# A graph layer with routed experts on one core: VectorE's chains reordered and shortened, block numbers loaded two at a time, TensorE's order kept

## What is computed

```
n = layernorm(x)
summed = segment_sum(n[src], dst);  deg = count of edges into a node
z = concat([n, summed / max(deg, 1)]) @ gnn_weight          # 512 -> 256
x1 = x + z / norm(z) + gnn_bias
h = layernorm(x1);  probs = softmax(h @ gate_w + gate_b);  e = argmax(probs)
pos = running count of the nodes that chose e;  kept = pos < 977
y = (relu(h @ w1[e] + b1[e]) @ w2[e] + b2[e]) * probs[e] * kept
out = x1 + nan_to_num(y)
```

## Time and profile before

| | us |
|---|---|
| median of 3 runs (lowest to highest) | 1400.24 (1398.0 to 1404.33) |
| profiled execution | 1398.44 |
| its span in the trace | 1396.6 |
| PE busy / DVE busy / POOL busy / ACT busy | 1120.8 / 868.0 / 907.4 / 464.5 |
| trips 0 to 7 (start of the first row store to that of the ninth) | 89.3 to 282.0 |
| trips with quads and a chunk | about 261 to 1245 |
| late trips, then trips with a chunk alone | to 1310, to 1396.6 |

### The profile page before, as it was taken

The page is one execution under the profiler, slowest core; times in us unless marked ns, Lnnn a source line. Parts: engine busy times, 40 slices in busy tenths (PEclk is TensorE's granted clock), DMA queues, the critical chain, the costliest instruction groups (busy, mean ns, idle before and its releaser), DMA issues.

```text
span 1396.6 us, 29269 instructions
## 1 busy us (share of the span) xinstructions
PE 1120.8 (80%) x4989; PEld 820.2 (59%) x4990; DVE 868.0 (62%) x3856; ACT 464.5 (33%) x1360; POOL 907.4 (65%) x931
## 2 busy tenths in 40 slices
PE   1076766788889898989888898989898888887786
PEld 1054554566666666666666666666666666654454
DVE  8645454666666666666666666666666666665443
ACT  3511212233333333333333333333333333334342
POOL 3167676677777777777777777777777777731101
PEclk9999798999999999999999999999999999999999
DMA  7686878443444434343433434343434344321111
GB/s 246 199 269 206 249 226 243 148 127 116 131 123 123 130 118 133 115 132 114 128 115 112 121 110 121 110 126 110 125 110 121 114 113 120 113 75 43 47 38 35
DMA packets 113601, 183.38 MB, mean 131 GB/s; under 512 B 21419, under 2 KB 84448, under 8 KB 113584
## 3 DMA queue, kind: packets, MB, share of 16 engines
q0 software_dynamic: 43328, 109.52, 27.2%
q1 hardware_dynamic: 70256, 73.69, 17.6%
HBM read 155.29 MB, written 35.83 MB: 137 GB/s over the span
## 4 chain that ended last, share of the span: by engine, by line
DVE 29%; PE 27%; DVEq 20%; issue 18%; DMA 3%; ACT 2%; ACTq 0%; SPq 0%; POOLq 0%; POOL 0%
PE ps_q L726 14%; PE ps_h L792 7%; DVE sel L1037 6%; DVEq L1301 6%; PE ps_t L800 2%; PE ps_b L811 2%; DVE acc L1046 2%; DVEq L1108 2%; DVEq L894 2%; DMA b_b<-in_L_ffn_b 2%; DVEq L1037 1%; DVEq L1064 1%; DVE row L1150 1%; DVE idx L1033 1%; DVE bn L1156 1%
## 5 line engine op out<-in xcount | busy, mean ns | idle before, releaser
L461 POOL DMA_INDIRECT ring<-xn_d,idx x784 | 788.0, 1005 | 316.5 <-issue 171.5
L726 PE MATMUL ps_q<-ring,sel 128*128 128x257 f32 x1952 | 582.8, 405 | 151.2 <-DVE sel L1037 119.9
L726 PEld LDWEIGHTS ps_q<-ring,sel 128*128 128x128 f32 x1952 | 346.5, 195 | 291.5 <-issue 234.3
L1037 DVE SCALAR_TENSOR_TENSOR sel<-lane,block,dst_t 128x512 f32<-128x512 bf16 x245 | 184.3, 752 | 132.8 <-issue 76.6
L811 PE MATMUL ps_b<-w_sb,hid_t 128*128 x832 | 213.8, 385 | 16.1 <-ACT hid_t L626 16.1
L1046 DVE TENSOR_TENSOR acc<-acc,ps_q 128x257 f32 x245 | 103.2, 421 | 178.4 <-issue 166.9
L792 PE MATMUL ps_h<-w_sb,hid_t 128*128 x416 | 200.0, 608 | 6.2 <-ACT hid_t L594 6.2
L811 PEld LDWEIGHTS ps_b<-w_sb,hid_t 128*128 128x128 f32 x832 | 153.5, 190 | 49.0 <-issue 30.1
L621 ACT ACTIVATE hid<-ps_h 128x512 f32<-128x512 f32 x104 | 62.1, 597 | 190.4 <-PE ps_h L792 190.4
L626 ACT ACTIVATE hid_t<-ps_t,b_t 128x128 f32<-128x128 f32 x416 | 113.2, 383 | 31.5 <-PE ps_t L800 31.5
L792 PEld LDWEIGHTS ps_h<-w_sb,hid_t 128*128 128x128 f32 x416 | 75.5, 191 | 67.4 <-issue 65.2
(11 more groups left out here) (194 smaller groups left out, 1230.0 us busy)
## 6 DMA issues: line engine op xcount, KB each, us to landing
w_sb<-in_L_ffn_w SPq DMA_DIRECT2D x32, 512.0 KB, 9.7
ring<-xn_d,idx POOLq DMA_INDIRECT x784, 2.8
disp_d<-hid SPq DMA_DIRECT2D x8, 1040.0 KB, 7.9
xs<-disp_d SPq DMA_DIRECT2D x53, 130.0 KB
ys<-disp_d SPq DMA_DIRECT2D x53, 130.0 KB
b_b<-in_L_ffn_b SPq DMA_DIRECT2D x53, 128.0 KB
xb<-in_x SPq DMA_DIRECT2D x51, 128.0 KB
out<-row SPq DMA_DIRECT2D x51, 128.0 KB
```

The source lines that it names most:

```text
L461: pool.indirect_dma_start(ring[:, (k % 2) * TQ + j, 0:D], None, xn_d[:, :], bass.IndirectOffsetOnAxis(ap=idx[:, k * TQ + j:k * TQ + j + 1] ...
L726: mm = pe.matmul(ps[:, 0:AW], sel[:, s, j, :], ring[:, (k % 2) * TQ + j, 0:AW], start=(j == 0), stop=(j == TQ - 1), skip_group_check=True)
L1037: dve.scalar_tensor_tensor(out=sel[:, s, :, :], in0=lane[:, :].rearrange("p (j m) -> p j m", j=1).to_broadcast((P, TQ, P)), scalar=block0[ ...
```

## The change

Work is moved between VectorE and ScalarE, and within VectorE's order. `plan`, TensorE's order of steps, keeps its entries, but for the loads of block numbers.

- `finish_row` leaves `result` and goes, with `choose`, into one set of chains with `new_row`, behind `select_quad`(3). `route` is alone behind `select_quad`(1), `result` alone behind `select_quad`(2).
- `down` waits for a new semaphore `count_read`, which the second step of `finish_row` raises, in place of `row_ready`.
- `route` has 5 steps in place of 9 (negated logits, the winner by the minimum before the exponentials), `result` 7 in place of 8 (the bias is scaled by ScalarE, `out_bias`), `new_row` loses its correction step: ScalarE's `row_norm` does that in four small operations. The copy of `row` to `sent` and the conversion of the edge indices `idx` go to ScalarE (`exponent`, `gather_rows`); VectorE's `quad_rows` goes.
- Each engine loads two block numbers for a quad: VectorE behind each selection, TensorE at one step of each quad.
- ScalarE prepares the next node block at the end of its trip, ahead of the copy that `gate` waits for; the normalised rows get a tile of their own, `xl`.
- In trips with a chunk alone ScalarE's `out_bias` stands between the two `hidden` copies.

```diff
             def exponent(t):
...
+                act.activation(sent[:, :], row[:, :], ACT.Copy).then_inc(exp_ready, 1)
...
-            def trip(t, chunk=True):
+            def trip(t, chunk=True, next_known=None):
                 c = chunks(t)
-                act.load([blk], ntab[0:1, ds(t, 1)])
                 act.wait_ge(xl_ps, t + 1)
                 act.activation(cat_t[:, 0:KD, :], ps_a[:, 0:KD, :], ACT.Copy).then_inc(xlt_ready, 1)
-                prepare_node(t, act.snap(blk, min_val=0, max_val=NB - 2))
+                gather_rows(t, 1)
...
+                    out_bias(c)
                 exponent(t)
                 row_norm(t)
                 if chunk:
-                    hidden(c, e)
+                    hidden(c, 0)
+                act.wait_ge(count_ps, t + 1)
+                gather_rows(t + 1, 0)
+                if chunk:
+                    hidden(c, 1)
+                    relus(c, e)
                 next_row(t)
...
+                prepare_node(t + 1, next_known)
...
                             if prev:
-                                pe.wait_ge(row_ready, t + 1)
+                                pe.wait_ge(count_read, t + 1)
...
-                        [steps((prev, counts), (chunk, up, 1), (quads, load_quads)),
+                        [steps((prev, counts), (chunk, up, 1), (quads, load_quad, 3)),
                          steps((chunk, hid_transposes, 0)),
                          steps((chunk, hid_transposes, 1)),
                          steps((chunk, down, (0, 1)))],
...
                 select(q, k % 2, to)
+                dve.load(ends_of, qtab[0:1, ds(t * QS + k + 1, 1), :])
...
                     dve.tensor_tensor(g8[:, 6, :], g8[:, 6, :], hot[:, :], ALU.mult)
-                    dve.tensor_tensor(seen[:, :], ps_b[:, D + EX:D + 2 * EX], seen[:, :], ALU.add)
+                    dve.tensor_tensor(seen[:, :], ps_b[:, D + EX:D + 2 * EX], seen[:, :], ALU.add
+                                      ).then_inc(count_read, 1)
...
                     add_last(t, 0)
                     select_quad(t, 1)
-                chains(route(t) if prev else [], choose(t, whole=prev) if chunk else [],
-                       send_copy(t) if prev else [])
-                if quads:
+                    chains(route(t))
                     add_last(t, 1)
                     select_quad(t, 2)
-                chains(result(t, node) if chunk else [],
-                       ([nothing] if chunk else []) + finish_row(t) if prev else [])
-                if quads:
+                    if chunk:
+                        chains(result(t, node))
                     add_last(t, 2)
                     select_quad(t, 3)
...
+                    chains(new_row(t, known), choose(t) if chunk else [], [nothing] + finish_row(t))
                     add_last(t, 3)
...
                     normalise_row(t)
...
                     select_quad(t + 1, 0)
...
                     prepare_node(t + 1, next_known)
```

More of the change, by code:

```diff
@@ L654, in trip @@
                 if chunk:
-                    hidden(c, e)
+                    hidden(c, 0)
+                act.wait_ge(count_ps, t + 1)
+                gather_rows(t + 1, 0)
+                if chunk:
+                    hidden(c, 1)
+                    relus(c, e)
                 next_row(t)
-            with act.Fori(0, C0) as t:
+                prepare_node(t + 1, next_known)
+            prepare_node(0)
+            trip(0, chunk=False)
+            with act.Fori(1, C0) as t:
                 trip(t, chunk=False)
@@ L757, in load_expert, with load_quad @@
                     expert.append(pe.snap(code[1], min_val=0, max_val=EX - 1))
-                def load_quads():
-                    pe.load(next_regs, qtab[0:1, ds(t * QS + QS, QS), :])
-                def turn_quads():
-                    for now, then in zip(regs, next_regs):
-                        pe.reg_mov(now, then)
+                def load_quad(k):
+                    pe.load(ends_of, qtab[0:1, ds(t * QS + k, 1), :])
                 def cat_transposes():
@@ L843, in steps @@
                     return run
-                plan = [[steps((prev, gate), (chunk, load_expert)),
+                plan = [[steps((prev, gate), (chunk, load_expert), (quads, load_quad, 1)),
                          steps(),
@@ L848, in trip @@
                          steps()],
-                        [steps((node, linear, 0)),
+                        [steps((node, linear, 0), (quads, load_quad, 2)),
                          steps((node, linear, 1)),
@@ L856, in trip @@
                          steps((chunk, down, (0, 1)))],
-                        [steps((chunk, down, (2, 3))),
+                        [steps((chunk, down, (2, 3)), (quads, load_quad, 4)),
                          steps((chunk, down, (4, 5))),
                          steps((chunk, down, (6, 7))),
-                         steps((node, xl_transposes), (quads, turn_quads))]]
+                         steps((node, xl_transposes))]]
                 if quads:
@@ L1169, in normalise_row @@
                 dve.drain().then_inc(stat2_ready, 1)
-            def send_copy(t):
-                def copy():
-                    if not isinstance(t, int):
-                        dve.wait_ge(disp_out, 16 * t)
-                    dve.tensor_copy(sent[:, :], row[:, :])
-                return [nothing, copy]
             def route(t):
@@ L1295, in s7, with trip @@
                     dve.sem_inc(res_ready, 1)
-                return [s0, s1, s2, s3, s4, s5, s6, s7]
-            def trip(t, quads=True, node=True, prev=True, chunk=True, next_node=True, next_known=None):
+                return [s0, s2, s3, s4, s5, s6, s7]
+            def trip(t, known=None, quads=True, node=True, prev=True, chunk=True, next_node=True, next_known=None):
+                if known is None:
+                    known = dve.snap(blk, min_val=0, max_val=NB - 2)
                 if quads:
-                    dve.load(next_regs, qtab[0:1, ds(t * QS + QS, QS), :])
                     dve.wait_ge(cat_ready, t + 1)
@@ L1304, in trip @@
                     select_quad(t, 1)
-                chains(route(t) if prev else [], choose(t, whole=prev) if chunk else [],
-                       send_copy(t) if prev else [])
-                if quads:
+                    chains(route(t))
                     add_last(t, 1)
                     select_quad(t, 2)
-                chains(result(t, node) if chunk else [],
-                       ([nothing] if chunk else []) + finish_row(t) if prev else [])
-                if quads:
+                    if chunk:
+                        chains(result(t, node))
                     add_last(t, 2)
                     select_quad(t, 3)
-                    for now, then in zip(regs, next_regs):
-                        dve.reg_mov(now, then)
-                if node:
-                    new_row(t)
-                if quads:
+                    chains(new_row(t, known), choose(t) if chunk else [], [nothing] + finish_row(t))
                     add_last(t, 3)
-                if node:
                     normalise_row(t)
-                if quads:
                     select_quad(t + 1, 0)
-                if node and next_node:
                     prepare_node(t + 1, next_known)
+                else:
+                    chains(route(t) if prev else [], choose(t, whole=prev) if chunk else [])
+                    chains(result(t, node) if chunk else [], finish_row(t) if prev else [])
+                    chains(new_row(t, known) if node else [])
+                    if node:
+                        normalise_row(t)
+                        if next_node:
+                            prepare_node(t + 1, next_known)
             dve.wait_ge(const_in, 16 * 4)
             prepare_node(0)
-            dve.load(regs, qtab[0:1, 0:QS, :])
+            dve.load(ends_of, qtab[0:1, 0:1, :])
             select_quad(dve.snap(n), 0)
```

175 lines of the change are left out of this document (95 added, 80 removed).

## The result

The changed kernel takes 1587.21 us (median of 4 runs, 1583.77 to 1588.2), beside 1399.12 us (4 runs, 1397.47 to 1404.33) for the kernel before: 1.133 times as long, 95% interval 1.130 to 1.137. The profiled execution has a span of 1586.2 us, 189.6 more than before.

What follows compares the result with a forecast made beforehand. GpSimd, almost without pause, was taken to bound the trip (23.8 of 23.90 us). 1398.4 + 108 + 83 - 10 + 5 = 1584.4, and 1.8 us for the runs' median: 1586 us, range 1550 to 1632 (chance 0.66).

Steps and rivals of the forecast that it cites:

- the main stretch: The 36 trips with a second visit in quad 3: +108 us for the hold and +83 for the clock.
- the first 8 trips: Trips without down: gain from the shorter load, loss at gate; -10 us, bounds -25 and +8.
- Held at quad 2's end: TensorE's down waits for count_read behind quad 3's selections: 4.55 us later, 4.8 us idle, in 36 trips.
- Given back: Selection waits vanish, loads and copy add 0.53 and 0.1 us at gate; 3.0 us net loss a trip, +108 us.
- the early end of VectorE's chain: VectorE's 8 rounds behind count_read end by 815.8 us, so gate waits only 0.1 us for ScalarE's copy.
- The clock: TensorE's clock halves behind each 4.8 us pause: 2.3 us a trip, +83 us in 36 trips, bounds 0 and +108.
- Rival (1): TensorE is held at quad 2's end but its clock does not fall, or seldom: 1503 us; chance 0.17.
- Behind the last quads: Chunk-alone trips: out_bias behind the first hidden copy delays results that hang together through ys; +5 us, bounds 0 and +8.
- 0 for the trips without a second visit: Five chunk trips with no second visit in quad 3: no change, held by GpSimd's 23.8 us.

Runs made afterwards that it cites:

- e5: Changed kernel with ScalarE's order put back alone: gate's copy first in its trip, node block prepared behind it; 1552.39 us beside 1404.85, ratio 1.104.
- e2: Changed kernel with five unused products between quad 2's end and the first down; three runs on other, slower chips, ratios 1.021, 1.017 and 1.037.
- e8: Changed kernel with count_read raised earlier, the first two steps of finish_row and choose ahead of new_row's chain; 1522.71 us beside 1404.85, ratio 1.085.
- e1b: Changed kernel with the order of VectorE's chains put back, the rest of the change kept; on a slower chip 1646.24 us beside 1652.25, ratio 0.997.
- e3: Changed kernel with down(0, 1) moved from quad 2's last step to quad 3's first; on a slower chip 1635.51 us beside 1631.57, ratio 1.004.
- e7: Kernel before, unaltered, traced on one of the slower chips; one execution, 1647.19 us.

## Why the prediction was right

Predicted 1586 us, measured 1587. That the number is off by 1 us is in part luck: the main stretch came out 16 us under its forecast, and the first 8 trips (13 us) and the end (6 us) above theirs. The mechanism is the predicted one. Step by step:

**Held at quad 2's end**: right in place, count and size. 4.81 us of idle time in 36 trips (predicted 4.8), `seen` as the releaser, 4.58 us more than before (4.55). `down`'s wait begins with the visit's end because VectorE has only then the slot for its selections, and the pieces that the prediction laid end to end (807.08 to 811.65) are there: selection to L1154's end is 808.11 - 803.72 = 4.39 us, 4.47 in the prediction's sum.

**Given back**: both waits for selections went. From `gate` to quad 2's end it is 1.30 us less (10.21 + 4.59 - 9.30 - 4.20), although the loads show there with 0.79 us behind `gate`; predicted were 1.32 + 0.1 - 0.53 = 0.89. The 0.76 us at quad 0 went too, but `gate`'s wait for ScalarE's copy, 0.48 us, came in their place. This term was mis-sized: I took 0.1 us a trip out of 0 to 0.9, and e5 shows 0.5. The step that failed is the early end of VectorE's chain, 815.8 us at the latest, taken as set by VectorE's own rounds: in the trace the selection is at 816.37 us, because the addition of quad 3's first visit, at 813.98, had waited 3.61 us for TensorE. The chain behind it moves with the hold and the clock, and with it the copy (at the full clock, in e2, it still waited 0.98 us).

**The clock**: it fell in 36 of 36 pauses, and it costs TensorE 8.74 or 9.85 less 7.05 us, 1.7 or 2.8 us, 2.25 on average; predicted 2.3. Whether the kernel loses that much depends on what `gate` would do at the full clock. By e2's undisturbed trips it is 8.54 us from `down` to `gate`, so the changed kernel's trip would be 4.81 + 8.54 + 9.30 + 4.20 = 26.85 us (an estimate from two kernels, e2's part from another chip) beside 24.05 before and 29.0 on average now: 2.8 us for the hold and 2.15 for the clock, for 36 trips 101 and 77 us. Predicted were 108 and 83, and the stage, forecast at 191, brings 175.1. By e8's trips without a fall (9.46 us) the split would be 134 and 44, but there VectorE's chain is late by its own steps, in e2 it waits for TensorE as in the changed kernel, so e2 is the nearer one. Rival (1), no fall, had 1503 us; by e2 it would be about 1510. No run at the place where the kernel before takes 1400 us has the pause without the fall, so this split is worked out and not measured as a time.

**The first 8 trips**: -10 predicted, +3.2 measured, within the bounds but of the other sign. TensorE's waits for selections there fell from 21.1 to 5.6 us, as expected. What failed is `gate` again: it waits 8 times, 10.7 us in all, as here:

```profile
189.01 0.44 PE L855 MATMUL ps_a<-ident,xl 128*128 128x128 f32 x2 [2.41 <-ACT xl L665]
190.16 1.22 PE L767 MATMUL ps_q<-ring,sel 128*128 128x257 f32 x2 [0.71 <-DVE sel L1069]
192.44 1.02 PE L861 MATMUL ps_b<-gatew_sb,cat_t 128*128 128x8 f32 x4 [1.06 <-ACT cat_t L671]
```

With e5's edit alone this stage ends at 275.92 us, 6.1 us ahead of before.

**Behind the last quads**: +5 predicted, +11.3 measured. The late trips, at 0 in the prediction, bring 4.6 (row stores 20.1, 16.6 and 18.0 us apart, 16.6, 16.7 and 16.8 before); with VectorE's order put back the first of them is 16.4 (e1b, on another chip). In the trips with a chunk alone the reason was wrong: one lasts 10.16 us in both kernels. The time goes where `out_bias` waits for the transfer of the bias, with the second `hidden` copy behind it (ScalarE's waits from 1495 to 1580 us):

```profile
ACT b_b L622 <- DMA b_b<-in_L_ffn_b: 12.3, 6, 7.7
```

**0 for the trips without a second visit**: right in size. They last 23.3 to 24.1 us, beside 22.6 to 24.1 before. That GpSimd holds them is not shown: in the first four of these five trips it has 0.7 to 1.15 us of idle time beyond its 0.30 us ahead of each transfer, where the usual trip of before has 0.2, and `gate` waits 0.92 us for ScalarE's copy.

## What to carry over

Before a step is moved behind another on one engine, look at what the *other* engine's queue has standing ahead of that step's consumer: a wait in the middle of a queue costs the sum of both engines' work, not the longer of the two, and moving the consumer (e3) can repair it as well as moving the producer. What a fallen clock costs depends on what the engine's next wait hangs on: if the other engine's chain waits for the slowed engine too, the loss stays whole (the changed kernel, by e2); if that chain is late by itself, part of it is time that would have been waited anyway (e8). So look first whether that chain's first step has waited for TensorE. And measure the kernel before on the same chip each time: a ratio of 1.13 was 1.04 where the engines came late to their instructions.

## What the runs showed of the hardware

On five of the chips that the runs were made on the kernel before took 16 to 18% longer, with transfers and operations as long as ever. There VectorE's and SyncE's plain register and branch instructions, mostly under 0.1 us each and only once above 0.25 in the first trace (0.30), took 0.25 us and more 271 times in e7 (181 us in all), most of them about 0.7 us, and ScalarE came to its copy up to 5.7 us late. It looks as though the engines' instructions arrive late; what makes them late was not tried and stays open. A load of two values into registers took 0.51 us at VectorE, nearly as long as at TensorE before (0.53).
